# Next state's transposes moved ahead on SyncE, gate quarters and low halves moved to VectorE

## The reference

```python
# layer 0: attention over the graph, 6 heads of 128
h = relu(layernorm(x))
q, k, v = h @ Wq + bq, h @ Wk + bk, h @ Wv + bv
probs = softmax(q k^T / sqrt(128) + where(adj, 0, -9e15))
x = x + (probs v) @ Wf + bf
# layer 1: graph attention, 12 heads of 64, and a gate
h = relu(layernorm(x))
hw = h @ W                                  # per head
attn = tanh(hw) @ w_src + (tanh(hw) @ w_dst)^T
attn = softmax(where(adj, leaky(attn, 0.2), -999))
f = elu(attn hw + b)
gate = sigmoid(h @ H_w.T + H_b)
x = x + gate * f + (1 - gate) * h
```

## Time and profile before

| | |
|---|---|
| time, median of 3 runs (lowest to highest) | 2587.43 us (2586.86 to 2588.43) |
| the profiled execution: its time; its span | 2591.12 us; 2589.1 us |
| mean granted TensorE clock | 0.984 |
| busy, share of the span: TensorE, VectorE | 94%, 84% |
| busy, share of the span: ScalarE, GpSimd | 44%, 39% |

### The profile page before, as it was taken

The page is one execution under the profiler, slowest core; times in us unless marked ns, Lnnn a source line. Parts: engine busy times, 40 slices in busy tenths (PEclk is TensorE's granted clock), DMA queues, the critical chain, the costliest instruction groups (busy, mean ns, idle before and its releaser), DMA issues.

```text
span 2589.1 us, 58735 instructions
## 1 busy us (share of the span) xinstructions
PE 2434.9 (94%) x22408; PEld 1720.3 (66%) x22439; DVE 2169.2 (84%) x3120; ACT 1149.9 (44%) x1528; POOL 998.8 (39%) x649
## 2 busy tenths in 40 slices
PE   7897999999999999999999999999999999999997
PEld 6664766666766666766667666667666667666665
DVE  7867888888888888888888888888888888888868
ACT  6434434444434444434444434444444444444434
POOL 0234423444333444333444234443234443344431
PEclk9999999999999999999999999999999999999999
DMA  7377666767676766666776666776667666767662
GB/s 251 99 179 214 166 195 166 205 205 192 180 195 166 210 209 178 189 180 183 211 206 168 199 169 198 208 196 176 193 169 212 205 189 185 197 167 212 205 160 50
DMA packets 755674, 481.25 MB, mean 186 GB/s; under 512 B 611760, under 2 KB 636336, under 8 KB 755632
## 3 DMA queue, kind: packets, MB, share of 16 engines
q1 hardware_dynamic: 755632, 480.65, 66.6%
HBM read 277.59 MB, written 34.60 MB: 121 GB/s over the span
## 4 chain that ended last, share of the span: by engine, by line
issue 31%; DVE 24%; SPq 12%; ACT 12%; POOL 8%; PE 6%; DMA 6%; POOLq 0%; ACTq 0%; DVEq 0%
SPq L671 6%; SPq L665 6%; DMA w_lo<-forms 4%; DVE p_place L1625 3%; PE pair_prj L1181 2%; DVE arena L1535 2%; DVE bn_out L1422 2%; DVE arena L1543 2%; PE pair_prj L900 2%; DVE arena L1532 2%; POOL arena L2674 2%; ACT arena L2162 2%; POOL arena L2623 2%; POOL arena L2628 2%; ACT arena L2444 2%
## 5 line engine op out<-in xcount | busy, mean ns | idle before, releaser
L900 PE MATMUL pair_prj<-w_hi,arena 128*128 128x256 f16 (+1 forms) x3432 | 806.6, 325 | 16.6 <-DVE p_place L1600 7.8
L900 PE MATMUL pair_prj<-w_lo,arena 128*128 128x256 f16 (+1 forms) x1716 | 557.9, 325 | 0.0
L900 PEld LDWEIGHTS pair_prj<-w_hi,arena 128*128 128x128 f16 x3432 | 335.9, 98 | 244.8 <-issue 20.6
L926 PE MATMUL pair_prj<-arena,w_hi 128*128 128x256 f16 x2376 | 394.2, 273 | 4.6 <-issue 2.5
L926 PE MATMUL pair_att<-arena,w_hi 128*128 128x256 f16 x2160 | 360.0, 273 | 0.0
L926 PE MATMUL pair_prj<-arena,w_lo 128*128 128x256 f16 x1188 | 324.7, 273 | 0.0
L2597 POOL TENSOR_TENSOR rstd<-var_eps,minus_half 128x2 f32<-128x2 f32 x62 | 87.2, 1407 | 543.7 <-DVE var_eps L1435 534.0
L926 PE MATMUL pair_att<-arena,w_lo 128*128 128x256 f16 x1080 | 294.4, 273 | 0.0
L1227 PE MATMUL pair_prj<-w_hi,arena 128*128 128x384 f16 x870 | 262.2, 335 | 11.3 <-DMA w_lo<-forms 9.5
L926 PEld LDWEIGHTS pair_prj<-arena,w_hi 128*128 128x128 f16 x2376 | 228.7, 98 | 31.6 <-issue 3.1
L900 PEld LDWEIGHTS pair_prj<-w_lo,arena 128*128 128x128 f16 x1716 | 168.1, 98 | 108.0 <-issue 0.6
(11 more groups left out here) (272 smaller groups left out, 5289.9 us busy)
## 6 DMA issues: line engine op xcount, KB each, us to landing
w_hi<-forms SPq DMA_DIRECT2D x353, 288.0 KB, 4.0
w_lo<-forms SPq DMA_DIRECT2D x353, 288.0 KB, 4.7
arena<-in_x SPq DMA_DIRECT2D x63, 768.0 KB, 4.7
out<-arena SPq DMA_DIRECT2D x64, 384.0 KB, 3.2
arena<-arena SPq DMA_DIRECT2D x31, 768.0 KB, 3.5
arena<-arena SPq DMA_TRANSPOSE x372, 3.2
forms<-w_lo SPq DMA_DIRECT2D x14, 288.0 KB, 3.5
forms<-w_hi SPq DMA_DIRECT2D x10, 288.0 KB, 4.0
```

The costliest lines, as they stand in the source:

```text
L900: mm = nc.tensor.matmul(pair[:, lo:hi], lhs(a, k), weight(m, k, b)[:, lo:hi], start=(k == 0 and n == 0), stop=(k == KT - 1 and n == 2))
L926: mm = nc.tensor.matmul(pair[:, c * 256:(c + 1) * 256], weight(m, k, a)[:, o:o + P], (ht0_hi, ht0_lo)[b][:, k, :], start=(k == 0 and n == ...
```

## The change

SyncE issues the transposes of the next state in the loop before it loads x1 and transposes the probabilities, and no longer after. VectorE now reads all seven gate products itself (`gate_quarter`): the first four with the bias row or a scaled partial sum, so that ScalarE's copies and GpSimd's gate biases go, and TensorE waits for VectorE's count `g_ready`. The low half of the next state is made by VectorE between its second `low_values` and `normal0`. K's second half is read before `output_first(1)`, `offset` stands between `output_elu` and `output_gated`, ScalarE's `h_from_kept(0)` stands before the normalisation, and GpSimd's output biases stand behind the products. In pass 2, which prepares the gate's forms, the stores of four quarters come later and the terms are made earlier.

```diff
@@ SyncE
                 if now and mid:
                     sp.dma_start(keep, x1).then_inc(x1_moved, DMA)
+                    if seven_gate(j):
+                        after_held(sp, transposes_held, v_psum, 2 * i + 2)
+                        transpose_rows(0, 0, ht0_hi, i + 1)
+                        transpose_rows(0, 1, ht0_lo, i + 1)
                     after_alone(sp, eye_made, full_made[1], 2 * j + 2)
                     after_alone(sp, eye_made, x1_moved, DMA * (2 * j + 2))
                     sp.dma_start(x1, x_g[i]).then_inc(x1_moved, DMA)
...
-                if nxt:
+                if nxt and not (mid and seven_gate(j)):
                     after_held(sp, transposes_held, v_psum, 2 * i + 2)
...
                 elif third:
-                    store_gate_quarters()
                     store_gate_highs()
...
                 elif third:
+                    store_gate_quarters()
                     gate_residents()
@@ TensorE, gate_form
                     elif n == 2:
-                        pe.wait_ge(gate_copied, 4 * s + 1)
+                        pe.wait_ge(g_ready, g_before(j) + 1)
...
                     elif n == 6:
-                        pe.wait_ge(gate_summed, 3 * s + 2)
+                        pe.wait_ge(g_ready, g_before(j) + 5)
@@ VectorE
+                def gate_quarter(form):
+
+                    t, half, made = {0: (0, 0, 0), 1: (1, 1, 0), 2: (1, 0, 0), 3: (0, 0, 1), 4: (1, 1, 2),
+                                     6: (0, 1, 0), 5: (1, 0, 3)}[form]
+                    dve.wait_ge(g_psum, g_before(j) + form + 1)
+                    if made:
+                        dve.wait_ge(g_ready, g_before(j) + made)
+                    else:
+                        dve.wait_ge(y_ready, 2 * p + 2)
+                    nc.vector.scalar_tensor_tensor(gate[:, t, columns(half)], gate_place(form), col(w_undo, WG),
+                                                   gate[:, t, columns(half)] if made else bg_row[:, columns(half)],
+                                                   ALU.mult, ALU.add).then_inc(g_ready, 1)
...
-                if last:
+                if last and not (mid and seven_gate(j)):
                     output_first(1, p)
                 if now:
                     dve.wait_ge(k_psum, 2 * i + 2)
                     biased_columns(1, pair_prj[1], kt, bk_col, col(w_undo, WK), k_ready)
+                if last and mid and seven_gate(j):
+                    output_first(1, p)
...
                 if last:
-                    output_last(1, p)
+                    output_elu(1, p)
                 if nxt and not second:
                     offset(0, i + 1)
+                if last:
+                    output_gated(1, p)
...
                     if nxt and not second:
                         low_values(1)
+                        low_part(0, 0, 2 * i + 1)
+                        low_part(0, 1, 2 * i + 2)
                     normal0()
...
                     h_target(0)
+                    gate_quarter(0)
                     h_low(1)
+                    gate_quarter(1)
                     h_source(1)
+                    gate_quarter(2)
                     h_target(1)
                     split_source_and_target()
-                    add_gate(0)
+                    gate_quarter(3)
                     context_low(0)
-                    add_gate(1)
+                    gate_quarter(4)
                     for n in (0, 2, 1, 3):
                         whole_sums(n)
                     spread_over_heads(0)
                     spread_over_heads(1)
-                    add_gate(2)
+                    gate_quarter(6)
+                    gate_quarter(5)
                     low_sums(2, 1)
@@ ScalarE
                 if last:
                     p1_high(1, p)
+                if last and seven_gate(j):
+                    h_from_kept(0, p)
                 if mid:
                     act.wait_ge(shift_ready[1], j + 1)
...
-                if mid and seven_gate(j):
-                    copy_gate(0)
-                    copy_gate(1)
-                    copy_gate(2)
@@ GpSimd
-                    if nxt and not second:
-                        low_part(0)
-                        low_part(1)
                     products(0)
-                    if early:
+                    if early and not seven_gate(j):
                         add_output_bias(0)
                     products(1)
                     if early:
+                        add_output_bias(0 if seven_gate(j) else 1)
+                    target_terms()
+                    if early and seven_gate(j):
                         add_output_bias(1)
-                    target_terms()
...
-                    if seven_gate(j):
-                        add_gate_bias(0)
-                        add_gate_bias(1)
```

More of the change, by code:

```diff
@@ L699, in first_forms @@
                 def first_forms():
-                    sp.wait_ge(forms_stored, GATE_STORED)
+                    sp.wait_ge(forms_stored, GATE_TERMS_STORED)
                     for n, form in ((1, B11), (2, B21), (3, T3), (0, T2)):
@@ L704, in gate_forms @@
                 def gate_forms():
+                    sp.wait_ge(forms_stored, GATE_STORED)
                     for n, form in enumerate((B11, T3, T2, B21)):
@@ L981, in project_h @@
                         if t:
-                            pe.wait_ge(g_ready, 2 * p + 2)
+                            pe.wait_ge(g_ready, g_before(p) + 2)
                     else:
@@ L1190, in form_product @@
                         pe.wait_ge(ct_ready, 2 * g + 1)
-                        if seven_gate(g - 1):
-                            pe.wait_ge(gate_summed, 3 * (g - 3) + 1)
-                        else:
-                            pe.wait_ge(g_ready, 2 * g)
+                        pe.wait_ge(g_ready, g_before(g - 1) + 4 if seven_gate(g - 1) else g_before(g - 1) + 2)
                     elif n == 1:
                         if seven_gate(g - 1):
-                            pe.wait_ge(gate_copied, 4 * (g - 3) + 4)
+                            pe.wait_ge(g_ready, g_before(g - 1) + 6)
                         else:
@@ L1202, in form_product @@
                         if seven_gate(g - 1):
-                            pe.wait_ge(gate_summed, 3 * (g - 3) + 3)
+                            pe.wait_ge(g_ready, g_before(g - 1) + 7)
                         else:
@@ L1237, in project_output @@
                     elif closing:
-                        pe.wait_ge(g_ready, 2 * j + 1)
+                        pe.wait_ge(g_ready, g_before(j) + 1)
                     elif mid and t == 0:
@@ L1242, in project_output @@
                     elif mid:
-                        pe.wait_ge(g_ready, 2 * j + 2)
+                        pe.wait_ge(g_ready, g_before(j) + 2)
                     else:
@@ L1717, in low_gate_term @@
                     dve.wait_ge(weight_hi, made_high(GATE_TERM, form))
-                    dve.wait_ge(terms_summed, 8)
+                    dve.wait_ge(terms_summed, 7 if form in (T1, T3) else 8)
                     nc.vector.scalar_tensor_tensor(gate_t_low[form], gate_term_of[form], col(w_scale, WG),
@@ L1744, in state_lows @@
                                                 state_high[pair], ALU.subtract).then_inc(state_sums, 1)
-                def add_gate(n):
-                    t, half = ((0, 0), (1, 1), (1, 0))[n]
-                    dve.wait_ge(g_psum, g_before(j) + 4 + n)
-                    dve.wait_ge(gate_copied, 4 * (j - 2) + 1 + n)
-                    nc.vector.scalar_tensor_tensor(gate[:, t, columns(half)], gate_place(3 + n), col(w_undo, WG),
-                                                   gate[:, t, columns(half)], ALU.mult, ALU.add)\
-                        .then_inc(gate_summed, 1)
+                def gate_quarter(form):
[9 more added lines that the diff above has]
+                                                   ALU.mult, ALU.add).then_inc(g_ready, 1)
                 def low_term(form):
@@ L2012, in one @@
                     variance(0, rows, i + 1)
+                if isinstance(i, int) and i == 2:
+                    for form in (T1, T3, T2):
+                        low_gate_term(form)
                 if last:
-                    output_last(1, p)
+                    output_elu(1, p)
                 if nxt and not second:
                     offset(0, i + 1)
+                if last:
+                    output_gated(1, p)
                 if isinstance(i, int) and i == 2:
-                    for form in (T1, T3, T2, T4):
-                        low_gate_term(form)
+                    low_gate_term(T4)
                 if now:
@@ L2322, in high_state @@
                         .then_inc(state_hi, 1)
-                def copy_gate(n):
-                    t, half = ((0, 0), (1, 1), (1, 0), (0, 1))[n]
-                    form = (0, 1, 2, 6)[n]
-                    act.wait_ge(g_psum, g_before(j) + form + 1)
-                    if n == 0:
```

(24 more changed lines are left out.)

15 lines of the change are left out of this document (4 added, 11 removed).

## The result

The changed kernel takes 2500.93 us (median of 4 runs, 2498.76 to 2501.55) against 2587.93 us before (4 runs): ratio 0.9658, 95% interval 0.9641 to 0.9675. The profiled execution has a span of 2499.3 us and a mean granted clock of 0.992.

A forecast was written before the change was run, and what follows sets the result against it. VectorE's order, stretched by GpSimd's SBUF instructions, was taken to stand behind TensorE's waits. Terms summed to -1.7, so 75.7 us a pass against a mean of 78.43; 28 times 2.7 is 76, giving 2511 us, range 2490 to 2530.

The forecast's parts named there:

- eight steps of the table: Lateness added between VectorE landmarks, shift to next shift: +1.8, -1.6, +1.0, -1.4 + 1.8, -0.6, +0.4 - 0.7, +0.6 - 1.6, -1.4 us.
- shift: VectorE's instruction before the normalisation, held by GpSimd's earlier add_h(0): +1.8 us a pass.
- the two low halves with the subtraction: Next state's low halves on VectorE, +1.8 us; softmax subtraction beside them no longer stretched, 2.37 to 0.96, -1.4.
- the attention output: With K's second half read ahead of output_first(1), it and the elu behind come later: +1.0 us a pass.
- the rival with shift free: VectorE's shift is not held up, TensorE's 74 us rule: 74.2 us a pass, 2469 us; chance 0.14.
- The late form: Load TensorE awaits before a gate product, 2.4 us a pass; would land at 1265.9 instead of 1270.57, ending VectorE's 1.60 wait.
- The clock: Granted clock in the loop passes: 1.00 expected throughout, where one of two neighbouring passes had 0.98.
- The tie: VectorE's softmax multiplication, reached after 7.1 us, against GpSimd's product after 7.0 to 7.2; leaned to VectorE first.
- the rival with GpSimd first: GpSimd's product precedes the softmax multiplication, which ends 1.7 us later: 77.4 us a pass, 2558 us; chance 0.24.
- The low halves: VectorE's new work +1.8 us, softmax subtraction -1.4, covered wait for the high half -0.6, longer stretch at probabilities' low half +0.4.
- the output biases: GpSimd's output bias runs behind the second pair of products instead of ahead, the tanh being ready earlier: -0.7 us a pass.
- The gate's biases and reads: GpSimd's bias adds go, low sum 1.98 to 0.55, -1.4 us; VectorE's fourth new quarter read +0.6, three others covered.

The follow-up runs named there:

- shift freed: The changed kernel with one wait more, so that GpSimd's add_h(0) starts only when VectorE's shift of the same pass is done: 2455.46 us.
- the first two experiments: Changed kernel with GpSimd's add_h(0) waiting for VectorE's shift, 2455.46 us; changed kernel with h_from_kept(0) back behind the normalisation, 2500.55 us.

## Why the prediction was right

The forecast was 2511 us, 2.7 us a pass; measured were 2500.93, 3.3 a pass.

- **The terms.** All eight steps of the table have the forecast's sign and are within 0.21 us of its size. They add up to -2.37 where the forecast had -1.7, since nearly all the misses lie on one side. The largest misses are shift (+1.59 for +1.8), the two low halves with the subtraction (+0.20 for +0.4) and the attention output (+0.86 for +1.0), all of them taken too dear. TensorE's own work, put at 74.0, was too dear as well: with shift freed the passes take 73.47, where the rival with shift free had 74.2 and 2469 us.
- **The late form.** Right: the second half is issued 24.9 us after the scores (1221.85 less 1196.94), where it was 28.4 (1267.17 less 1238.79) and the forecast 23.7, and no wait is left. TensorE's new wait is 1.45, not 1.0 to 1.2: it holds all that TensorE is idle in a pass (75.06 less 73.61), of which the forecast had put a few tenths elsewhere.
- **The clock.** Right: 1.00 in the passes. That the lower level comes from TensorE's long waits is only argued. In the loop before, the stretches at 1.2 GHz came right behind waits for a form of 2.1 us or more, in the run without SyncE's order and in the one with it alone behind waits of 1.95 or more, and the changed kernel, which waits 1.45, has none. But a wait of 2.85 before 2210.94 of the kernel before had none behind it, so the length of the wait alone does not settle it.
- **Who holds whom.** Right at all four places named: shift held (1.76), subtraction of the state free (0.55), softmax subtraction 0.96, low sum 0.55. For shift and the state's subtraction the first two experiments show it by moving one add to three places; for the softmax subtraction the run with the low halves on GpSimd does (2.02), for the low sums the one with the gate sums as before (1.49 and 1.64). The row that the prediction gave for reads of PSUM (0.62 at 1266.22) stands beside no long GpSimd instruction that reads SBUF; the reading holds all the same: 0.94 at 1216.12, beside the product of 1215.34, against 0.95 at 1245.35, where GpSimd was idle. The Trainium skill, SBUF — State Buffer, section Who interferes with whom, says that of two instructions that get in each other's way the one that is issued first blocks the other; the trace agrees in both directions: `add_h(0)`, 0.07 earlier, holds shift, and VectorE's multiplication of 1212.75 makes the product of 1212.99 take 2.39 where it took 1.81.
- **The tie.** VectorE's multiplication was first, by 0.24 us, as leaned to; the rival with GpSimd first did not come.
- **The low halves.** Forecast as +1.8 - 1.4 - 0.6 + 0.4, nearly nothing, and measured as nothing. The Trainium skill, Perfetto Trace Analysis, section Optimizing Scalar/DVE Operations, says that moving work between these two engines might not help; for the low halves the runs agree (2499.65 against 2500.93 us). For the gate's biases it does not carry over: there VectorE took on 4 instructions that read PSUM in place of adds that hold it for 2.0 us a pass when they are put back, and 43.5 us came of it.
- **What the forecast did not see.** It put the output biases at -0.7, through an earlier tanh, and asked of the load of x1 only what it does to the probabilities. Under the new order of SyncE the bias waits for x1, and its move is worth 2.0 us a pass. That the sum does not show this is luck, because both edits were in the change. By its terms the change without the bias move would take 2511 + 28 x 0.7 = 2531 us, and it took 2556.63; for the new order alone the same reasoning gave 2509 to 2526 us, and it took 2583.39. The gate's biases and reads it put at -1.4 + 0.6, 22 us, where undoing them costs 43.5: under the new order two low sums are held, where in the pass before one was (1.98).

## What to carry to other kernels

When a transfer is moved ahead in a queue, list also the transfers that it pushes back and follow each to the instruction that waits for it and to what stands behind that one: here the new order gained 8 us while a bias add that waits for such a load stood in its old place, and about 70 once it was moved. In these traces a GpSimd instruction of 128 by 768 elements that reads SBUF costs VectorE nothing where VectorE reads PSUM (0.94 us at 1216.12), reduces one operand (0.94 at 1216.99, 0.95 without GpSimd) or takes its statistics (1.93 at 1197.23, 1.94 without GpSimd), or waits for a third engine. It costs up to 1.6 us where VectorE combines two operands in SBUF, and 1.27 at the scaling `var_eps`. So one wait that moves it can be worth as much as moving work between the two: 45.5 us here, against 43.5 for the gate sums and nothing for the low halves. The value of an edit depends on which engine sets the pace: K's order costs 26 us in the changed kernel and nothing once TensorE is the bound.

## What the runs showed that was not expected

The parts do not add up. SyncE's order alone gains 8 us, all the rest without it 3 or nothing, and both together 87. An instruction of VectorE on 128 by 2 elements can lose as much as one on 128 by 384: shift takes 1.76 instead of 0.16, which the forecast had counted on, and `var_eps` 1.44 instead of 0.17, which it had not. Both end with GpSimd's add. With one wait added, TensorE ran through whole passes with 0.05 us not busy in 73.47, while VectorE was busy for 67.10.
